# Cross attention of a decoder layer: probabilities made in turned form, row maxima carried as contraction rows, output finished one loop body later

## The reference, cut to what matters

```python
def _L0_xattn_ref(q, v, k, Wq, bq, Wk, bk, Wv, bv, Wo, bo):   # NH = 16 heads, DK = 32
    qh = (q @ Wq.T + bq).reshape(b, s, NH, DK).transpose(0, 2, 1, 3)
    kh = (k @ Wk.T + bk).reshape(b, s, NH, DK).transpose(0, 2, 1, 3)
    vh = (v @ Wv.T + bv).reshape(b, s, NH, DK).transpose(0, 2, 1, 3)
    scores = jnp.einsum('bhqd,bhkd->bhqk', qh, kh) / jnp.sqrt(DK)
    probs = jax.nn.softmax(scores, axis=-1)
    ctx = jnp.einsum('bhqk,bhkd->bhqd', probs, vh)
    return ctx.transpose(0, 2, 1, 3).reshape(b, s, h) @ Wo.T + bo
x = x + _L0_xattn_ref(_layernorm(x, axis=-1), ctx_1024, ctx_1024, ...)
```

## Time and profile before

| what | us |
|---|---|
| median of 3 executions | 2903.49 (2901.74 to 2908.31) |
| the profiled execution, own time | 2908.36 |
| its span, first to last instruction | 2906.7 |
| TensorE busy / VectorE / ScalarE / GpSimd | 2509.3 / 1661.9 / 1373.6 / 581.4 |
| mean granted TensorE clock | 0.928 of full |

### The profile page before, as it was taken

How to read it: one execution, slowest core, us unless ns; L and a number is a source line. 1 busy time by engine, 2 the same in 40 slices (tenths; PEclk the granted TensorE clock), 3 DMA queues, 4 the chain that set the end, 5 groups by cost and what they waited for, 6 DMA issues and landing times. The chain is left out here.

```text
span 2906.7 us, 48839 instructions
## 1 busy us (share of the span) xinstructions
PE 2509.3 (86%) x16612; PEld 2224.2 (77%) x16612; DVE 1661.9 (57%) x3202; ACT 1373.6 (47%) x2868; POOL 581.4 (20%) x770
## 2 busy tenths in 40 slices
PE   4999999999974887787788887329999999999996
PEld 4999999999974676676676765228888888898885
DVE  6787878878852765675676675544333433333331
ACT  5555656556532654564465555014443434344442
POOL 1111111111102332333233331111202112022011
PEclk9999999999986999899899997559999999999998
DMA  3101001010106565565555553042324323234231
GB/s 104 38 24 38 30 23 44 23 44 23 38 29 166 143 152 127 126 162 137 131 141 141 138 142 77 15 112 87 101 74 126 90 96 98 90 95 109 76 76 18
DMA packets 232228, 254.51 MB, mean 88 GB/s; under 512 B 68264, under 2 KB 158376, under 8 KB 231440
## 3 DMA queue, kind: packets, MB, share of 16 engines
q1 hardware_dynamic: 190992, 231.17, 29.2%
q0 software_dynamic: 40960, 20.41, 4.0%
HBM read 182.47 MB, written 68.80 MB: 86 GB/s over the span
## 5 line engine op out<-in xcount | busy, mean ns | idle before, releaser
L1884 ACT ACTIVATE d_hf<-d_psH,d_b1c 128x308 f32<-128x308 f32 x256 | 130.8, 517 | 411.0 <-PE d_psH L1783 411.0
L1781 PE MATMUL d_psH<-d_xgT_h,d_w_l 128*128 128x308 f32 x1024 | 317.1, 310 | 7.0 <-issue 5.6
L1908 DVE TENSOR_TENSOR d_h_l<-d_hf,d_h_h 128x616 fp32r<-128x616 f32 x128 | 101.9, 799 | 385.3 <-ACT d_h_h L1853 385.3
L303 PE MATMUL a_psP<-a_xnT_h,a_win_l 128*128 128x256 f32 x1024 | 304.7, 298 | 15.2 <-DVE a_xnT_l L540 14.3
L1782 PE MATMUL d_psH<-d_xgT_l,d_w_h 128*128 128x308 f32 x1024 | 313.1, 306 | 0.0
L1783 PE MATMUL d_psH<-d_xgT_h,d_w_h 128*128 128x308 f32 x1024 | 312.7, 305 | 0.0
L1187 ACT ACTIVATE b_pr<-b_psS,b_nm 128x256 f32<-128x256 f32 x512 | 235.3, 481 | 133.0 <-DVE b_nm L1297 132.9
L304 PE MATMUL a_psP<-a_xnT_l,a_win_h 128*128 128x256 f32 x1024 | 296.3, 289 | 0.0
L305 PE MATMUL a_psP<-a_xnT_h,a_win_h 128*128 128x256 f32 x1024 | 295.1, 288 | 0.0
L1781 PE MATMUL d_psO<-d_w_h,d_h_l 128*123 128x512 f32 x640 | 253.7, 396 | 9.3 <-DVE d_h_l L1908 9.3
L1782 PE MATMUL d_psO<-d_w_l,d_h_h 128*123 128x512 f32 x640 | 253.4, 396 | 0.0
(11 more groups left out here) (317 smaller groups left out, 6468.9 us busy)
## 6 DMA issues: line engine op xcount, KB each, us to landing
d_w<-in_W_dram SPq DMA_DIRECT2D x64, 1024.0 KB, 7.2
b_qst<-qs_d SPq DMA_DIRECT2D x48, 512.0 KB, 9.2
b_kst<-ks_d SPq DMA_DIRECT2D x48, 512.0 KB, 7.0
a_xl<-in_x_dram SPq DMA_DIRECT2D x16, 512.0 KB, 4.3
a_xres<-in_x_dram SPq DMA_DIRECT2D x16, 512.0 KB, 3.8
x_d<-a_xres SPq DMA_DIRECT2D x16, 512.0 KB, 3.1
b_xa<-x_d SPq DMA_DIRECT2D x16, 512.0 KB, 4.5
b_cx<-in_ctxT_dram SPq DMA_DIRECT2D x16, 512.0 KB, 12.0
```

What stands on the lines that cost most here:

```text
L303: pe.matmul(out, lo_w, hi_x, start=first, stop=False)
L1781: pe.matmul(out, lo_w, hi_x, start=first, stop=False)
L1884: act.activation(hf[:, m % 2, n * HALF:(n + 1) * HALF], psH[n][:, 0:HALF], ACT.Silu, bias=b1c[par][:, m:m + 1]).then_inc(silu_s, 1)
```

## The change

The softmax is computed without turning the probabilities. The scores of 128 queries by 256 keys are still computed (`scores`), but only for their row maxima. POOL splits the maxima into a high and a low part and puts them into columns 96 to 103 of an otherwise empty tile `mxp` (`max_parts`); TensorE turns that tile (`turn_max`, two transposes for each four heads), and ACT writes the eight rows, negated and repeated for four heads, under the 96 rows of the stacked queries (`max_rows`, `qst` rows 96 to 103). The stacked keys carry ones in the rows that belong to their head. A second product (`turned`, 104 contraction rows, keys stationary) then gives scores minus maximum with the keys on the partitions, ACT takes the exponential of four heads in one instruction straight into `PT`, and `pv` multiplies with the values and, in 16 matmuls more of the same shape, with a tile of ones, which gives each row's sum in the other half of `psV`. DVE takes the reciprocal of the 256 sums on all partitions and multiplies (`ctx_f`).

Further: `t_f` is gone; ACT writes the biased queries and keys straight into `t_l`, and POOL makes `t_h` from it and subtracts in place, so ACT, and no longer POOL, waits for the stores of tile i-2 (`q_f`). All softmax steps of entry b stand in body b+1, the last product with the values and the output projection in body b+2. The context's parts are made one by one in the body that uses them. SP loads the residual at the start of a body and stores the router's rows at its end. The diff, cut to its core:

```diff
-        t_f = sb("t_f", [P, 2, S])
+        qst = [sb(f"qst{i}", [KX, H, S], F32R) for i in range(2)]
+        kst = [sb(f"kst{i}", [KX, H, S], F32R) for i in range(2)]
...
-        pr = sb("pr", [P, 2, G, S])
+        PT = sb("PT", [P, 2, G, TT, S])
+        mx, mxp = sb("mx", [P, TT, G]), sb("mxp", [P, 2, TT, P], F32R)
+        cf = sb("cf", [P, S])
...
+                if prev2:
+
+                    wait(sp, x2_st, 16 * (b - 2))
+                    sp.dma_start(xres[:], x1_v[b - 2]).then_inc(xres_ld, 16)
...
+                    load(qs_d, tq_st, q_ld, qst[par], (0, 1, 0))
                 if prev2:
...
+                    sp.wait_ge(x2_s, 2 * (b - 1))
+                    sp.dma_start(y_v[b - 2], xres[:]).then_inc(x2_st, 16)
...
+                def max_parts(i):
...
+                    g.tensor_copy(mxp[:, j % 2, qt, KR:KR + G], mx[:, qt, :]).then_inc(mh_s, 1)
+                    pool.wait_ge(mh_s, n + 1)
+                    g.tensor_tensor(mxp[:, j % 2, qt, KR + G:KX], mx[:, qt, :], f32(mxp[:, j % 2, qt, KR:KR + G]),
+                                    ALU.subtract).then_inc(ml_s, 1)
...
+                for i in range(U):
                     if cur:
...
+                        qk_parts(i)
+                    if prev:
+                        max_parts(i)
+                    if cur and i < KD:
+                        cx_part(i)
...
+                def turn_max(j):
+
+
+                    pe.wait_ge(ml_s, U * (b - 1) + 2 * j + 2)
+                    for qt in range(TT):
+                        mm = pe.transpose(psS[1][:, 0, qt * P:(qt + 1) * P], f32(mxp[:, j % 2, qt, :]), ident[:])
...
+                    elif j < KD - 1:
+                        pe.wait_ge(exp_s, U * (b - 1) + 2 * j + kt)
+                    if kt == 0:
+                        pe.wait_ge(mr_s, KD * (b - 1) + j + 1)
+                    if j == 2 and kt == 0 and prev2:
+                        pe.wait_ge(r_cp, b - 1)
+                    ps = psS[kt] if j == KD - 1 else psT
...
+                        mm = pe.matmul(ps[:, h, :], kst[o][0:KX, G * j + h, kt * P:(kt + 1) * P],
+                                       qst[o][0:KX, G * j + h, :], start=True, stop=True)
...
+                    for half_, w in enumerate((V[v], None)):
+                        for kt in range(TT):
+                            for h in range(G):
...
+                                mm = pe.matmul(psV[h * DK:(h + 1) * DK, half_ * S:(half_ + 1) * S],
+                                               ones[:] if w is None else w[:, kt, c], PT[:, j % 2, h, kt, :],
...
+                def q_f(i):
                     act.wait_ge(qk_mm, U * b + i + 1)
...
+                    if m >= 2:
+                        act.wait_ge((tq_st, tk_st)[n][m % 2], 64 * b + 32)
+                    elif n == 1:
+                        act.wait_ge(tq_st[m % 2], 64 * b + 64)
+                    else:
+                        wait(act, tk_st[m % 2], 64 * b)
+                    act.activation(f32(t_l[:, i % 2, :]), psQ[:, 0:S], ACT.Identity,
...
+                    act.activation(qst[o][KR:KX, G * j:G * j + G, :],
+                                   psS[1][KR:KX, 0, :].rearrange("p (o s) -> p o s", o=1).broadcast_to([2 * G, G, S]),
+                                   ACT.Copy, scale=-1.0).then_inc(mr_s, 1)
...
+                    act.activation(PT[:, j % 2, :, kt, :], ps[:], ACT.Exp, scale=SCALE).then_inc(exp_s, 1)
...
+                    dve.reciprocal(cf[:], psV[:, S:2 * S]).then_inc(rec_s, 1)
+                    dve.wait_ge(rec_s, n + 1)
+                    dve.tensor_tensor(cf[:], psV[:, 0:S], cf[:], ALU.mult).then_inc(cf_s, 1)
```

More of the change, by code:

```diff
@@ new lines, in body @@
+                if prev2:
+                    pv(b - 2, KD - 1, par)
+                if cur:
+                    qk_tile(2)
+                if prev:
+                    turn_max(0)
+                    scores(1, 0)
+                    turned(0, 0)
+                if cur:
+                    qk_tile(3)
+                if prev2:
+                    out_proj(0)
+                if prev:
+                    scores(1, 1)
+                    turned(0, 1)
+                if prev2:
+                    out_proj(1)
@@ new lines, in body @@
+                if prev:
+                    turn_max(1)
+                if cur:
+                    qk_tile(4)
+                if prev:
+                    scores(2, 0)
+                    turned(1, 0)
+                    pv(b - 1, 0, o)
+                if cur:
+                    qk_tile(5)
+                if prev:
+                    scores(2, 1)
+                    turned(1, 1)
+                if cur:
+                    qk_tile(6)
+                if prev:
+                    turn_max(2)
+                    scores(3, 0)
@@ L1121, in body @@
+                if prev2:
+                    turn_rows()
+                if prev:
+                    pv(b - 1, 1, o)
+                    turned(2, 0)
+                if cur:
+                    qk_tile(7)
+                if prev:
+                    scores(3, 1)
+                    turned(2, 1)
                 if cur:
                     v_tile(0)
+                if prev2:
+                    logits()
                 if prev:
-                    turn_p(U - 1)
+                    turn_max(3)
@@ L1190, in pt_copy @@
[L1190 to L1201 removed]
+                    m, n = i % KD, i // KD
@@ L1287, in body, with row_max @@
                 o = 1 - par
[L1289 to L1291 removed]
+                more = cur and not last(b)
+                def row_max(j, qt):
+                    n = U * (b - 1) + 2 * j + qt
                     dve.wait_ge(s_mm, n + 1)
[L1293 to L1297 removed]
@@ new lines, in body @@
+                if first(b):
+                    for c in range(2, 8):
+                        weights_lo(c)
+                if prev:
+                    row_max(0, 0)
+                    row_max(0, 1)
+                if prev2:
+                    ctx_f(b - 2, KD - 1)
+                if prev:
+                    row_max(1, 0)
+                if prev2:
+                    ctx_lo(b - 2, KD - 1)
+                    x2(0)
+                if prev:
+                    row_max(1, 1)
+                if prev2:
+                    x2(1)
+                    dve.wait_ge(x2_s, 2 * (b - 1))
+                    for t in range(TT):
+                        stats(b - 2, ln3, xres, st3, t)
+                    moments(b - 2, ln3, st3, mv3, ve3)
@@ new lines, in body @@
+                if prev:
+                    row_max(2, 0)
+                    ctx_f(b - 1, 0)
+                    ctx_lo(b - 1, 0)
+                    row_max(2, 1)
+                if prev2:
+                    wait(dve, xn3_st, 16 * (b - 2))
+                    normalize(b - 2, ln3, xres, mv3, rs3, rstd3, xn3)
+                if prev:
+                    row_max(3, 0)
+                if more:
+                    dve.wait_ge(xa_ld, 16 * b + 32)
+                    for t in range(TT):
+                        stats(b + 1, ln, xa, st, t)
@@ new lines, in body @@
+                if prev:
+                    ctx_f(b - 1, 1)
+                    ctx_lo(b - 1, 1)
+                    row_max(3, 1)
+                if more:
+                    moments(b + 1, ln, st, mv, ve)
+                if prev2:
+                    dve.wait_ge(r_mm, b - 1)
+                    for t in range(TT):
+                        ins = dve.tensor_tensor(lg[:, bass.ds((b * TT + (t - 2 * TT)) * NE, NE)],
+                                                psV[:, t * NE:(t + 1) * NE], brb[:], ALU.add)
+                    ins.then_inc(lg_s, 1)
```

394 lines of the change are left out of this document (178 added, 216 removed).

## The result

The changed kernel takes 2810.1 us (median of 4 executions, 2805.6 to 2813.1) where the kernel before takes 2902.6 (2898.9 to 2908.3): a ratio of 0.968, with a 95% interval of 0.966 to 0.970. It is 92 us faster; the forecast was 54. The profiled execution is one of 2813.1 us, with a span of 2811.5.

A forecast was written before the change was run, and what follows sets the result against it. TensorE was taken as the busiest engine, with the gain in its waits. From 2908.4, 50.7 us less in the bodies, 2 lost and 6 gained at the ends gave 2853.7 profiled, 2849 us median; range 2803 to 2905.

The forecast's parts named there:

- rival (1): Bodies: more overlap than walked, key tile's store in time and another wait gone; body 47.3 us, total 2810; chance 0.13.
- The gain of the bodies: Attention loop: 3.9 us less in each of 13 bodies, 50.7 us in all.
- The branch back: Loop's branch: VectorE late again, costing TensorE 5.5 us in each of five branches, 27 us, left unchanged.
- The waits of the walk: TensorE in a full body: waits 1.0 before qk 1, 0.9 turned (0,0), 1.4 turn_max 2, 1.8 turned (2,0).
- the sum of bytes: First key tile's store, queued behind loads and stores at 0.185 MB/us: lands after 14.3 us, holding ScalarE 4.2 us.
- The work: TensorE in a body: 43.8 us before, 8.2 of transposes removed, products and ones added, 45.0 us after.
- The reciprocal of 256 elements: VectorE's reciprocal of the row sums: 1.77 us, between bounds of 0.48 and 2.8.
- (3): Rival, VectorE: a dearer reciprocal of 2.2 us, counting at two waits, 1.0 us a body; 2862 us; chance 0.10.
- GpSimd's pair: GpSimd's small operations of 4 elements: 0.25 us each, 0.5 us for a pair.
- (2): Rival, handoffs: GpSimd's pairs at 1 us and a second wait of each kind; body 53.3, 2888 us; chance 0.15.
- (4): Rival, slower than before: stores hold in-order ScalarE; at a 20.5 us landing, body 56.5, 2930 us; chance 0.17.
- The ends: Outside the full bodies: 2 us lost in body 1 through later loads, 6 us gained in the tail.

The follow-up runs named there:

- e1: The kernel before with the six turns of its attention loop written out, so no engine branches back; 2880.8 us, ratio 0.990.
- e9: The kernel before with 16 semaphore increments on VectorE ahead of its loop; 2871.8 us, ratio 0.985.
- e10: The changed kernel with two groups of 42 semaphore increments added to each loop body on VectorE; 2847.5 us, ratio 0.977.
- e4: The changed kernel with VectorE's second maximum of step 2 ahead of the low part of context 0; 2802.2 us, ratio 0.962.
- e11: e8 with step 2's maxima write and router's copy ahead of tile 6's bias, and context 3's low part ahead of step 1's maximum; 2751.4 us, ratio 0.944.
- e6: e4 with the next context's load issued behind the keys' load, not ahead of the key tiles' stores; 2779.3 us, ratio 0.955.
- e2: The kernel before with an entry's first two scores moved behind query tile 0 of the next body; 2908.8 us, ratio 0.998.
- e8: e6 with turn_max 0 ahead of query tile 2, context 2's parts behind the next body's tile 0, and later selector casts; 2786.3 us, ratio 0.957.
- e7: The changed kernel with the products with ones over only the second half of the keys; 2813.4 us, ratio 0.966.
- e12: e11 with the products with ones over only the second half of the keys; 2744.0 us, ratio 0.942.

## Why the prediction was right, and where it was off

The sign and the mechanism (waits, not work) were right. Of the ranges, the one of the forecast itself (2825 to 2885) did not hold 2810; the whole one (2803 to 2905) did, since rival (1) had drawn its lower end. The gain of the bodies was put at 50.7 us and was 109.3; the 58.6 that are missing are these.

**The branch back, 27 us.** "I leave its 5.5 us as they are" was the step that failed. The reading of the earlier trace rows was right, but the cause was taken for something that every branch has. e1, e9 and e10 show what it was: the place of VectorE's loop among blocks of instructions, and the shorter program moved it.

**The waits of the walk, 23 us.** Walked: 1.0, 0.9, 1.4, 1.8, and 0.2 more. In 13 bodies: 0.4 (before `qk_tile(1)`), 1.0, 1.9, 0, and 0.1 for the keys, 3.5 for 5.3. TensorE in body 5 of the changed kernel, counted from query tile 0 at 1140.25:

```profile
1142.98 0.38 PE L1014 MATMUL b_psQ<-b_xnT_h,b_w_l 128*128 128x256 f32 x1 [0.65 <-ACT b_t_l L1270]
1150.34 0.74 PE L1109 MATMUL b_psT<-b_qst,b_kst 104*128 104x256 f32 x4 [0.99 <-ACT b_qst L1275]
1169.60 0.44 PE L1090 MATMUL b_psS<-b_ident,b_mxp 128*128 128x128 f32 x2 [1.95 <-POOL b_mxp L987]
```

turned (0,0) started at 10.1 (walked 10.2) and turn_max 2 at 29.4 (walked 29.4), so the chain VectorE, GpSimd, TensorE was right. The 1.8 us before turned (2,0) were not there. The key tile's store did hold ScalarE, as the sum of bytes had it, but it landed sooner:

```profile
1157.83 1.38 SPq L890 DMA_DIRECT2D b_qst<-qs_d  x3
...
1170.11 0.47 ACT L1270 ACTIVATE b_t_l<-b_psQ,b_bkc 128x256 f32<-128x256 f32 x1 [2.73 <-DMA ks_d<-b_t_l]
```

12.3 us behind the queries' load for the 14.3 of the sum (0.5 MB more at the sum's own 0.185 MB/us would even give 14.9): 165 GB/s in this body against 151 in body 3 of before. ScalarE waited 2.7 us for 4.2 and was free just when turn_max 2 had delivered. It was hidden with nothing to spare: e4 took the wait ahead of it away, and it stood there.

**The work, 16 us.** 45.0 us summed, 43.8 busy at the full clock. The turned products are 0.5 us each, not 0.56; a `turn_max` takes 0.14 of TensorE's time ahead of the scores behind it, not 0.25; a pv half is 0.9 to 1.0.

**The other way, 7 us.** Over all thirteen bodies TensorE is busy for 44.3 us each and not for 43.8: in four of them it fell to the half level right behind the wait of 1.94 us before turn_max 2 (clock 0.97, 1.5 us each). With 27 + 23 + 16 - 7 = 59 the account closes.

**What else was forecast.** The reciprocal of 256 elements: 1.77 us, from two rows of 4 and 32 elements. Measured (duration in ns, least, median, most):

```profile
L1418 DVE RECIPROCAL b_cf<-b_psV x64: 1740/1758/1758, 974.5 to 1716.2; 128x256 f32<-128x256 f32 x64
```

So (3) falls, and with it what the Trainium skill's repeat count gave (VectorE: DVE Perf Modes, section on the fixed hardware budget, 2.28 us). GpSimd's pair is 0.19 and 0.20 us, 0.5 with the gap: right, which excludes (2). ScalarE's exponentials and writes are 1.02: right. Its idle time before the bias of tile 2 is none: right. (4), the slower case, needed a landing of 18.5 us; it was 12.3. (1) named the body of 47.3 us and two conditions. One wait less came; the landing came earlier, but still 2.7 us behind the time at which q_f 6 wanted it. Its 2810 us is the time measured, by luck: it kept the 27 us of the branch, and the changed kernel lost others in their place, 7 in the bodies, 7 of scatter, and the rest at the ends.

**The ends.** Forecast +2 and -6, measured +7.1 (3.7 for the casts, 3.4 for bodies 0 and 1) and -1.4. The tail was to be shorter by six handoffs a step; it has single waits of 4.4 us before turn_max 2, 2.8 and 3.4 for the context's parts, and 4.6 for the normalized rows.

## What to carry over

A stall behind a branch with no releaser belongs to where a loop lies in its engine's program: before it is carried over to a changed program (or worked around), move the loop by a few instructions that do nothing. When an in-order engine waits for a store with work queued behind it, put the work that needs no store ahead; here that (e11), and taking a load out of the store's way (e6), stand in the two runs with the large gains. And once a body is balanced, an exchange that takes one wait away must be walked to the next engine that is late, or the wait only changes its place (e2, e4, e8).

## What the runs showed of the hardware

- VectorE came 4.2 to 5.7 us late behind a branch back when its loop held both of the places 960 and 1216 (two ends of the blocks in which instructions are fetched, by the page cited above), with about 5 instruction packets more for each branch, and was not late when the loop held one, at lengths up to 322. 16 idle instructions in the right place were worth 1.5% of this kernel, 1.0% of it seen in the loop's bodies.
- Less work on TensorE did not shorten the body while it waited for others: with 1.5 us less, its clock was below full in eleven bodies of thirteen, for four in the changed kernel (e7). In e11 and e12, with waits of up to 0.8 and 1.6 us, it stayed at 1.00.
- Two casts of 8 x 4096 elements took GpSimd 7.25 us and more than doubled the time of VectorE's subtractions beside them (5.74 for 2.51 us).
